# Transformer of four layers on one core: the first attention regrouped into 32-row scores, column-group outputs and GpSimd lowering

## What is computed

```python
q = split_heads(query @ Wq + bq)      # 16 heads of 8 features
k = split_heads(key @ Wk + bk)
v = split_heads(value @ Wv + bv)
scores = einsum('bhqd,bhkd->bhqk', q, k) / sqrt(8) + mask * -1e9
attn = softmax(scores, axis=-1)       # over 77 keys
x = einsum('bhqk,bhkd->bhqd', attn, v) # back to 128 features
return x @ Wo + bo
```

## Time and profile before

| | |
|---|---|
| runs before, us | 876.34, 875.88, 879.57 (median 876.34) |
| profiled execution: span from first to last instruction | 877.9 us |
| instructions | 15816 |
| PE / PEld busy | 757.7 us (86%) / 616.2 us (70%) |
| DVE / ACT / POOL busy | 538.3 (61%) / 518.1 (59%) / 291.1 (33%) us |
| mean granted TensorE clock | 0.943 of full speed |

### The profile page before, as it was taken

One profiled execution on the slowest core, in us unless ns is written; L12 is line 12 of the kernel. 1 busy time (PEld: TensorE's weight loads), 2 busy tenths in 40 slices (PEclk: granted clock), 3 DMA queues, 4 the chain that ended last, 5 costly groups with the idle time before them and its releaser, 6 DMA issues.

```text
span 877.9 us, 15816 instructions
## 1 busy us (share of the span) xinstructions
PE 757.7 (86%) x4663; PEld 616.2 (70%) x4663; DVE 538.3 (61%) x1919; ACT 518.1 (59%) x1751; POOL 291.1 (33%) x334
## 2 busy tenths in 40 slices
PE   3888878788888898899999899989999998876597
PEld 1566657666666477677997577778778875665597
DVE  4756657444454779765555897776233056886575
ACT  1878666345554888764556555568553348773275
POOL 4200031353552333543352344442000013243355
PEclk9999989868999999999999999999999999897599
DMA  7894477023324320000313890000000050000121
GB/s 234 211 205 196 121 222 162 28 87 81 83 62 121 147 73 1 14 13 27 80 49 121 208 214 15 1 1 1 1 0 1 1 187 6 1 16 10 50 70 50
DMA packets 35956, 69.57 MB, mean 79 GB/s; under 512 B 7121, under 2 KB 25809, under 8 KB 32033
## 3 DMA queue, kind: packets, MB, share of 16 engines
q1 hardware_dynamic: 30384, 57.98, 24.4%
q0 software_dynamic: 4768, 9.91, 3.3%
q10 hardware_dynamic: 720, 0.68, 0.3%
HBM read 58.45 MB, written 37.67 MB: 109 GB/s over the span
## 4 chain that ended last, share of the span: by engine, by line
PE 52%; DVE 17%; ACT 12%; issue 9%; POOL 6%; DMA 1%; another core or an unknown queue 1%; SPq 1%; POOLq 0%; DVEq 0%; ACTq 0%
PE bank L1226 10%; PE bank L1063 6%; PE bank L1094 6%; PE bank L1198 5%; ACT s_S L1892 4%; PE bank L1022 4%; PE bank L1077 3%; DVE s_xn L1388 3%; POOL out L2089 3%; PE bank L1092 3%; PE bank L1177 3%; PE bank L1171 2%; POOL xs_L L2082 2%; DVE s_peak L1425 2%; ACT s_S L1895 2%
## 5 line engine op out<-in xcount | busy, mean ns | idle before, releaser
L1063 PE MATMUL bank<-s_A,s_xTq 128*128 128x462 f32 (+1 forms) x352 | 149.1, 520 | 5.5 <-ACT s_S L1895 1.7
L2055 POOL TENSOR_TENSOR s_S<-s_S,s_inv 128x462 f32<-128x462 f32 (+2 forms) x123 | 100.4, 834 | 141.8 <-DVE s_inv L1439 140.2
L1077 PEld LDWEIGHTS bank<-s_ident,s_S 128*128 128x128 f32 (+2 forms) x560 | 67.9, 144 | 74.9 <-issue 39.2
L1077 PE MATMUL bank<-s_ident,s_S 128*128 128x128 f32 (+2 forms) x560 | 91.5, 284 | 26.7 <-POOL s_S L2055 11.8
L1915 ACT ACTIVATE s_PT<-bank 128x384 f32<-128x384 f32 (+1 forms) x176 | 82.6, 478 | 43.7 <-PE bank L1077 39.2
L1094 PE MATMUL bank<-s_VW,s_PT 128*128 128x128 f32 (+2 forms) x800 | 100.9, 282 | 0.0
L2082 POOL DMA_INDIRECT xs_L<-s_xn,s_sli x64 | 62.2, 971 | 116.2 <-DVE s_sli L1546 75.2
L1094 PEld LDWEIGHTS bank<-s_VW,s_PT 128*128 128x128 f32 (+2 forms) x800 | 96.9, 199 | 0.0
L1892 ACT ACTIVATE s_S<-s_S,s_peak 128x77 f32<-128x77 f32 x256 | 67.7, 351 | 7.0 <-DVE s_peak L1425 6.5
L1063 PEld LDWEIGHTS bank<-s_A,s_xTq 128*128 128x128 f32 x352 | 57.1, 199 | 17.4 <-issue 7.9
L1962 ACT ACTIVATE s_hT<-bank,s_b1T 128x128 f32<-128x128 f32 x184 | 52.3, 369 | 21.8 <-issue 9.1
(11 more groups left out here) (234 smaller groups left out, 1674.2 us busy)
## 6 DMA issues: line engine op xcount, KB each, us to landing
xs_L<-xs_L SPq DMA_DIRECT2D x24, 1122.0 KB, 30.9
s_xe<-xs_L SPq DMA_DIRECT2D x85, 66.0 KB
s_moe<-in_L_w SPq DMA_DIRECT2D x2, 2048.0 KB, 10.4
s_moe<-in_L_w SPq DMA_DIRECT2D x8, 512.0 KB, 7.4
s_yb<-ys_L SPq DMA_DIRECT2D x12, 256.0 KB, 3.0
s_arena<-in_L_w SPq DMA_DIRECT2D x2, 1024.0 KB, 6.1
s_arena<-in_L_h SPq DMA_DIRECT2D x2, 1024.0 KB, 9.2
s_b2bc<-in_L_b SPq DMA_DIRECT2D x2, 512.0 KB, 24.3
```

The source lines that it names most:

```text
L1063: mm(bank[b][:, 0:(h1 - h0) * KEYS], xTq_of(L, n)[:, i % 4, :], A[:, n, h0 * KEYS:h1 * KEYS], start=True, stop=True).then_inc(scores.up(L, ...
L1077: w = turn(bank[b][0:m, P * (t - t0):P * (t - t0) + P], S[s][:, P * t:P * t + m], ident)
L2055: p.tensor_tensor(val, val, rep(inv[s][:, h0:h1], KEYS, 2), ALU.mult).then_inc(normed.up(L, i, k), 1)
```

## The change

It regroups the first attention:

- `GROUPS[0]` becomes two halves of eight heads. The scores of a tile are one piece `S`: four products that each take 32 rows of q (four heads) and 308 columns of A, for rows 0, 32, 64 and 96, into banks 0, 1, 2 and 3. A keeps only 4 x 77 columns for each batch, with `hfour` in the place of `hmask`.
- `E` of a half: DVE adds the mask over two banks at once (616 elements) and takes the eight maxima. For half 0 ACT makes eight exponentials, one for each head, and each now also writes its sum. For half 1 POOL adds the negated maxima to all 616 elements (`lowered`), and ACT makes one exponential over them.
- The half is padded: 5 blocks of 128 columns for each, with zeros behind the 616. The transposes are ten whole ones in bunches of 4, 4 and 2.
- `O`: twelve products with 32 columns of the value matrix as weights and a turned block of exponentials moving (128 columns). Each of the four goes to its own 32 output partitions and takes three blocks, so the output arrives turned. Five more products give the sums of heads 8 to 15 (8 moving columns from `hk`). The sums of heads 0 to 7 come from ACT, whose eight exponentials now accumulate into `total`.
- `sum` (DVE) takes two reciprocals of eight; `spread` copies them out eightfold on POOL, turns that on PE (in the banks of `T`), and ACT copies it; `div` is then one multiplication on DVE that writes the turned, divided output, which `Wo` takes one turn later. `Ot` is gone. `Wo` also moves into the banks of `T`.
- The order of a turn is new (12 pieces instead of 14), an output is added two tiles back instead of three, and `finish` is rewritten to match. The pieces `xt`, `route`, `sigm` of routing group 2 are no longer put by hand in the last turn.

```diff
-GROUPS = ([(0, 6), (6, 12), (12, 16)], [(0, 6), (6, 12), (12, 16)], [(0, 6), (6, 12), (12, 16)], [(0, 6), (6, 8)])
+GROUPS = ([(0, 8), (8, 16)], [(0, 6), (6, 12), (12, 16)], [(0, 6), (6, 12), (12, 16)], [(0, 6), (6, 8)])
@@ first_order(s)
+        out = [("S", 0, 0, 0)] if s == 0 else []
+        if s:
+            out += [("T", 0, s - 1, q) for q in range(3)]
+        if s < NT:
+            out += [("E", 0, s, 0)]
+        out += live(s, ("div", 2), ("Wo", 2))
+        if s < NT:
+            out += [("E", 0, s, 1)]
+        out += live(s, ("add", 0, 2), ("O", 0, 1), ("sum", 1))
+        if s + 1 < NT:
+            out += [None] * ((s + 1) % 4 == 0) + [("S", 0, s + 1, 0)]
+        return out + live(s, ("spread", 1))
@@ finish(L), L == 0
+            now(("div", z - 1), ("Wo", z - 1), ("T", 0, z, 0))
             add(z - 1)
+            now(("T", 0, z, 1), ("T", 0, z, 2), *choice, ("O", 0, z), ("sum", z), ("spread", z), *rest[:1],
+                *norm("r", 3, 1, 2), ("div", z), ("Wo", z), *rest[1:], *late, *norm("r", 3, 3, 4, 5, 6, 7))
             add(z)
+            now(("xt", "r", 0, 3), *steps("route", 3, 0), ("sigm", 0, 3))
@@ tensor_program
+                    for j in range(4):
+                        w = mm(bank[j][:, 0:4 * KEYS], xTq_of(0, n)[32 * j:32 * j + 32, i % 4, :],
+                               A[32 * j:32 * j + 32, n, 0:4 * KEYS], start=True, stop=True)
+                        empty[j] = moved.at(0, i, j // 2)
+                    w.then_inc(scores.up(0, i, 0), 1)
...
+                    for r in range(3):
+                        for j, t in enumerate(FIRST_OF):
+                            w = mm(bank[b][32 * j:32 * j + 32, 0:P], VW[:, n, t + r, 32 * j:32 * j + 32],
+                                   PT[k][:, t + r, :], start=r == 0, stop=r == 2)
+                    for t in range(5):
+                        w = mm(bank[b][:, P:P + 8], PT[k][:, 5 + t, :], hk[:, t, :], start=t == 0, stop=t == 4)
...
+            elif kind == "spread":
+                pe.wait_ge(*wide_made.at(i))
+                turn(bank[b][:, 0:P], wide[i % 2], ident).then_inc(spread_sum.up(i), 1)
@@ vector_program
+                    half = S[s][:, HALF0 * k:HALF0 * k + 8 * KEYS]
+                    v.tensor_tensor(half.rearrange("p (a h k) -> p a h k", a=2, k=KEYS),
+                                    banks[:, 2 * k:2 * k + 2, 0:4 * KEYS].rearrange("p a (h k) -> p a h k", k=KEYS),
+                                    rep(rep(mk0[:, i % 4, :], 4, 1), 2, 1), ALU.add).then_inc(moved.up(0, i, k), 1)
+                    v.tensor_reduce(peak[s][:, h0:h1], half.rearrange("p (h k) -> p h k", k=KEYS), AX, ALU.max,
+                                    negate=True).then_inc(peaks.up(0, i, k), 1)
...
+            elif kind == "sum":
+                v.reciprocal(inv[s][:, 0:8], total[s][:, 0:8])
+                v.reciprocal(inv[s][:, 8:16], bank[bank_o["O", 0, i]][:, P:P + 8]).then_inc(inverted.up(i), 1)
             elif kind == "div":
+                v.tensor_tensor(oT[i % 2], bank[bank_o["O", 0, i]][:, 0:P], rs[i % 2],
                                 ALU.mult).then_inc(divided.up(i), 1)
@@ scalar_program
+                if L == 0 and k:
+                    act.wait_ge(*lowered.at(i))
+                    a(S[s][:, HALF0:HALF0 + 8 * KEYS], S[s][:, HALF0:HALF0 + 8 * KEYS],
+                      ACT.Exp).then_inc(probs.up(0, i, k), 1)
...
-                        if L == 0 or h0 < SUMMED[L]:
+                        if h0 < SUMMED[L]:
@@ gpsimd_program
+            elif kind == "E" and at[0] == 0 and at[2] == 1:
+                p.tensor_tensor(val, val, rep(peak[s][:, 8:16], KEYS, 2), ALU.add).then_inc(lowered.up(i), 1)
+            elif kind == "spread":
+                p.tensor_copy(wide[i % 2].rearrange("p (h d) -> p h d", d=8),
+                              rep(inv[nth[0, i] % 3], 8, 2)).then_inc(wide_made.up(i), 1)
```

More of the change, by code:

```diff
@@ L605, in ring @@
         return {p: banks[n % len(banks)] for n, p in enumerate(turn)}
[L607 to L608 removed]
+    banks = ctx.enter_context(nc.psum_tensor("bank", [P, 8, 512], F32))[:, :, :]
+    bank = [banks[:, i, :] for i in range(8)]
+    nth_s = [p for p in plan if p[0] == "S" and p[1] > 0]
     bank_s = {p: n % 4 for n, p in enumerate(nth_s)}
[L610 to L611 removed]
+    bank_t = ring(("xt", "wq", "T", "spread", "Wo"), (4, 5))
+    bank_o = {p: bank_s["S", p[1], NT - 1, 0] if p[1] and p[2] == NT - 2 else 6 for p in plan if p[0] == "O"}
     bank_k = ring(("k0", "v0", "vwt"), (0, 1, 2, 3))
@@ L619, in body @@
     OUT, MISC = 6, 7
-    bank_w = {i: MISC if i < NT - 4 else 3 for i in range(NT)}
     top = [-(-nc.sbuf_base // 64) * 64]
@@ L646, in body @@
     hmask = put("hmask", [P, 16])
-    hk = put("hk", [P, 10, 16])
+    hfour = put("hfour", [P, 4])
+    hk = put("hk", [P, 5, 8])
     iota8 = put("iota8", [P, 8])
@@ L724, in body @@
     yo = [*(yb[k][:, i, :] for k in (0, 1) for i in range(4)), *(put(f"yo{i}", [P, P]) for i in range(8, YO))]
-    Vbd = [put(f"Vbd{i}", [P, 16 * KEYS], at=at_m + 64 * KEYS * i) for i in range(2)]
+    Vbd = [put(f"Vbd{i}", [P, C0], at=at_m + 4 * C0 * i) for i in range(2)]
     VWT = put("VWT", [P, NB, 16 * KEYS], at=at_s)
@@ L882, in body @@
     filled, vbd_made = signal("filled", "init"), signal("vbd_made", "vbd")
+    lowered = signal("lowered", (a[1:2] for a in events("E") if a[0] == 0 and a[2] == 1))
+    wide_made = signal("wide_made", "spread")
     normed = signal("normed", ((L, i, k) for L, i, part in events("norm") for k in part_of(L, part)
```

194 lines of the change are left out of this document (85 added, 109 removed).

## The result

The changed kernel takes 882.59 us (median of five runs, 881.84 to 886.75) where the kernel before takes 876.34 (five runs, 875.76 to 879.57) on the same chip: ratio 1.0075, 95% interval 1.0057 to 1.0093. It is slower, and 867.0 was forecast. The profiled executions differ less than the medians: their spans are 880.8 and 877.9 us.

The account below looks back on a forecast made before the run. PE was taken to set the first attention's turn, ACT close behind. Loop 5.6 us less, drain 3.8 less, start 0.1 more: 9.3 off the 876.34 median gives 867.0 us, range 855 to 883.

Parts of the forecast that it names:

- I take 7.1, which is 6.56 and half a microsecond: Tile loop: a turn takes PE's 6.56 us with side work plus half a microsecond of mutual waiting; 7.85 before.
- the drain: Last tiles after the loop: two tiles deep instead of three, 9.5 us for 13.3, 2.2 of it for low clock.
- Scores and outputs, the bounds and the value taken: PE products: scores 1.28 us (bounds 0.51 and 2.05), twelve column products 1.44 (bounds 0.67 and 2.66).
- Column groups do not run beside each other: Rival: the twelve output products take 24 slots, 1.22 us more a turn; 888 us, 15 in 100.
- All four run beside each other: Rival: scores and outputs both fully overlap, PE falls by 1.5, DVE bounds a 6.4 us turn; 856 us, 12 in 100.
- The slot rule: PE scores and column products: each two-pass product adds one slot, so four take 5 slots and twelve take 13.
- PE sets the turn with ACT close behind.: Loop before: PE 6.85 us a turn, ACT 6.2, each making the other wait, 1.0 us up to 7.85.
- hidden: POOL's lowering (1.3 us a turn) hides under outputs and scores, the spread chain beside the 1.28 us of scores.
- The clock: Low PE clock: 1.5 us after each of two send stalls and 2.2 us in the drain.
- The sends: Turns 10 and 14: eight sends delay POOL's lowering and spreading copy, a 6 us stall each, turn 12.4 us.
- the nameless waits: Kernel before, ends of two send rows: DVE waits of 3.6 and 6.6 us without named cause, costing about 3.
- The waits take it: Rival: POOL's place in the loop costs 0.5 us more a turn and 3 more a stall; 874 to 881, 23 in 100.

Follow-up runs that it names:

- e1: Changed kernel with the copy that spreads the reciprocals moved from GpSimd to VectorE: 876.57 us, ratio 0.9985.
- e2: Changed kernel with the spreading copy on VectorE and the eight sends of a group issued two at a time, once a turn: 865.22 us, ratio 0.9857.
- e8: Changed kernel with the twelve column products ordered group by group instead of in turn over the four groups: 885.47 us, ratio 1.0111.
- e4: Changed kernel with the scores made from 128 rows again, and the mask product for the keys 1232 wide again: 898.8 us, ratio 1.0237.
- e3: Changed kernel without the lowering on GpSimd; eight exponentials on ScalarE for the second half of the heads: 896.4 us, ratio 1.0223.
- e13: Changed kernel run again unchanged, on a slow chip: ratio 1.0066 to the kernel before, last add at 176.74 us.
- e18: Changed kernel run again unchanged, on a fast chip: ratio 1.0275 to the kernel before, last add at 178.61 us.
- e12: Kernel before, run again unchanged on a slow chip for its profile: last add at 174.03 us.
- e17: Kernel before, run again unchanged on a fast chip for its profile: last add at 159.79 us.
- e14: The kernel of e2 run again unchanged, on a slow chip: 865.28 us, ratio 0.9842.
- e9: The kernel of e2 plus 48 unread transposes where TensorE idles ahead of a fall of the clock, on a fast chip: 845.67 us, ratio 0.9947.

## Why the prediction was wrong

**The step that failed is the turn: "I take 7.1, which is 6.56 and half a microsecond".** It measured 8.2. The last exponential ends at 164.47 us, so the loop took 140.5 us where 131.1 were forecast, and the drain 12.65 where 9.5 were. In the loop the two turns with sends took 25.7 us (forecast 7.1 twice and 15, 29.2). The other fourteen took 114.8, or 8.2 each, where 101.9 were left for them, or 7.3. This 12.9 is more than the stage's whole miss of 12.4 (last add at 177.12, forecast 9.3 before 174.01); the medians miss by 15.6, since the profiled execution of the kernel before was slower than its median. Bare turns were sized rightly, 7.28 us. The forecast spread the side work evenly, 0.93 us of PE a turn, and the six turns that carry it or the low clock take 9.78.

Why the turn is 8.2 and not 7.3. Only the copy and the sends were taken out by experiment (e1: 6 us, e2: both); the parts below are sized from traces, and they overlap, so that their shares of the 12.9 are not shown.

*Scores and outputs, the bounds and the value taken.* Wrong in size, to the good side. By pitch the scores are about 0.54 (0.80 less the last pass of 0.27) and the columns 0.66; the forecast's lower bounds, 0.51 and 0.67, were the truth. The rival "Column groups do not run beside each other" fails with that: it needed 24 slots, 2.66 us, and even e8's order takes 1.59. The rival "All four run beside each other" had the mechanism right, and so did the Trainium skill's page "TensorE: Matmul & The Clock Gate", section "Part 3: Packing small matmuls": its 3.07 gives 0.67 for the scores, and measured are 2.32 against 0.80 with the last pass, or about 3.8 by pitch. The slot rule from the 64-row products did not carry over to four groups. That rival's 856 failed for the same reason as the forecast: it let the whole gain through to the turn.

*"PE sets the turn with ACT close behind."* Half right. PE's time still counts (e4: an estimated 14 us of the 24 that 1.52 a turn add up to), and so does ACT's (e3: 14 of 21). As I read it, they take turns on one path, so a shorter PE piece shows only where PE was the last to come.

*POOL "hidden".* Half wrong. The lowering is hidden (ACT waits 2.2 us for it in the whole stage), but the spreading copy is not. Its cover was to be the 1.28 us of the scores; with scores of 0.80 PE comes to the spread early, and beside the value product and bias sum it waits 2.84 us. The text named this ("its cover goes if the scores get faster") and gave it no price.

*The clock.* Priced at 1.5 us behind each stall and 2.2 in the drain, and nothing elsewhere. Measured is a mean of 0.81 over the stage against 0.93 before; on a fast chip 0.78 against 0.99. An estimate from these: PE's busy time times the clock falls from 127.0 x 0.93 = 118 to 117.05 x 0.81 = 95 us, 23 less at full speed, of which 10 are left in busy time. One turn costs 2.8 us more at 0.59 than at 1.00 (e13), though these were given back. The drain runs at 0.69 where 0.79 was assumed. Its last turn takes 10.41 us at 0.66 here and 12.00 at 0.50 in e18, the same kernel, so a tenth of the clock is worth about 1 us there (an estimate). That is a third of the drain's 3.15 us of miss; the rest was not traced. Why the clock falls where it does is open.

*A cost that nobody listed.* DVE has small operations with two inputs from memory on chip, for the row norms. Beside GpSimd's products they last until those end:

```profile
68.59 0.68 DVE L1375 SCALAR_TENSOR_TENSOR s_nvr<-s_nvr 128x4 f32<-128x4 f32 x1 [1.03 <-ACT s_nvr L1851]
69.31 1.18 DVE L1379 TENSOR_TENSOR s_nvr<-s_nvr,s_nvr 128x4 f32<-128x4 f32 x1
```

GpSimd's value product above ends at 69.25 and its bias sum at 70.47; these two end at 69.27 and 70.49. Such operations took 0.15 to 0.16 us before; five of them here, these two and three near 51 us, lose 4.2 us together. The Trainium skill's page "SBUF — State Buffer", section "Who interferes with whom", says that a VectorE instruction with two inputs in that memory contends with a GpSimd instruction that reads it, and calls what they share an exclusive lock; the trace agrees, since both operations end with the GpSimd instruction beside them.

*ACT.* Summing exponentials were taken 0.30 apart, as in the second attention; here each is 0.25 and a read of the sum 0.09, so 0.34:

```profile
75.55 0.35 ACT L1908 ACTIVATE s_S<-s_S,s_peak 128x77 f32<-128x77 f32 x1
75.80 0.19 ACT L1908 ACTIVATION_READ_ACCUMULATOR s_S<-s_S,s_peak 128x1 f32 x1
```

That is 0.3 us a turn more. The exponential of 616 (0.70 to 0.72), the lowering (1.22), mask and maximum (0.79 and 0.80) were right within 0.02.

*A gain that nobody listed.* The forecast sized the smaller mask product for A but not where it lies. Two of them stand ahead of the first scores (0.86 us for both instead of 2.78), which start at 22.32 us instead of 23.71. The loop above is counted from 24, as in the forecast, so counted from its first scores it is 1.4 us longer still.

**The sends: right, to the place.** Three sends ahead of turn 10's lowering, five more ahead of its copy; again in turn 14. Turns of 12.4 us and 1.5 for the clock were forecast, 13.54 and 12.19 measured; the gap on PE is 7.63 in the first and 3.07 in the second, where PE was slow before it. Not foreseen: the first send waits 3.64 us for a transfer that clears its target, and GpSimd's queue, with the lowering in it, stands meanwhile. "I assume that the nameless waits fall inside these stalls" also held: none is left, and the changed stage is as long on fast chips, which have none. Their price was wrong: "cost about 3", where four turns of e12 with these waits and the clock behind them are 13 us longer than the same turns of e17. The sum took the loop before as measured, so this did not move the forecast.

**The comparison.** What the forecast could not see is that 14 us of the kernel before's stage belong to the kind of chip. Against an undisturbed kernel before the change costs 2.75%, not 0.75. The third rival, "The waits take it", is the mechanism that came nearest: it allowed 881 at worst, and 882.59 was measured; its 0.5 a turn was too little (0.9, and not all of it GpSimd's) and its 3 more a stall too much. That 882.59 lies inside the stated range of 855 to 883 is owed to that rival's end of it: the forecast itself had 861 to 872 and the other direction.

## What to carry to other kernels

A part that becomes cheap is worth what is left once the next thing on the path is late: before counting it, list for the new loop what stands ahead of each short operation in its queue, DMA issues too, and price it in the turns with side work and not in the bare turn. Keep what another engine waits for out of a queue that also issues long rows of transfers; sending two at a time in the gaps took off 12 us here, and moving the copy as well 17. And measure on more than one chip when the profile has waits without a name.

## What the runs showed of the hardware

- Two kinds of chip: 876 to 877 and 848 to 849 us for one kernel. 14 us of it lie in the stage, the nameless waits with the clock behind them; from the last add to the end it is 703 to 707 us on slow chips and 681 to 694 on fast chips. On slow chips there are nameless waits there too, on fast chips none; whether these are the whole difference was not looked into.
- The same loop of the same kernel has its low-clock turns in other places from run to run (e2 and e14: the stage at 0.86 and 0.77 of the clock); e1's ten runs span 869 to 880 us with a mean clock of 0.934 to 0.915.
- Twelve products on four column groups take 0.86 us when neighbours differ in group and 1.59 when they don't.
- The two versions fastest against the kernel before are e2 (0.9857 and 0.9842 on slow chips) and e9, the same with unread products (0.9947 on a fast one).
